# Token couplings folded into VectorE's updates: tanh + ratio times the values, then an addition with a factor

## The reference

```python
gf = _global_net(x.mean(axis=1, keepdims=True), ...)      # one number per batch
out = x
for _ in range(3):
    tf = _coupling_net(out, ...)                          # one number per token
    combined = 0.7 * gf + 0.3 * tf
    coupling = 0.1 + adaptive_range * (combined - 0.5) * 2.0
    out = out + coupling * _twist(out)                    # _twist permutes feature quarters, with signs
```

## Time and profile before

| what | value |
|---|---|
| median of 3 runs | 1072.22 us (1072.2 to 1073.6) |
| the profiled execution's own time | 1072.12 us |
| its span (first to last instruction) | 1070.2 us |
| what lies around the span | 1.9 us |
| mean granted TensorE clock | 0.983 of full speed |
| instructions | 21910 |

### The profile page before, as it was taken

The page is one execution under the profiler, slowest core; times in us unless marked ns, Lnnn a source line. Parts: engine busy times, 40 slices in busy tenths (PEclk is TensorE's granted clock), DMA queues, the critical chain, the costliest instruction groups (busy, mean ns, idle before and its releaser), DMA issues.

```text
span 1070.2 us, 21910 instructions
## 1 busy us (share of the span) xinstructions
PE 977.3 (91%) x7260; PEld 526.2 (49%) x7260; DVE 843.8 (79%) x1770; ACT 901.5 (84%) x1121; POOL 573.9 (54%) x1053
## 2 busy tenths in 40 slices
PE   6899999999899999999999999999989999996993
PEld 4456435554355544555445543555435554454431
DVE  3888796997879886987869879699796988688485
ACT  3999778997799978998789977899779997895575
POOL 3366604876068740887228870487606874087204
PEclk7999999999999999999999999999999999999897
DMA  5433002430033200432005310153002430020002
GB/s 118 88 59 58 6 2 44 103 88 1 1 75 89 71 1 1 98 89 48 1 1 118 88 30 1 36 112 88 0 2 69 92 74 1 2 54 31 11 1 80
DMA packets 191119, 51.71 MB, mean 48 GB/s; under 512 B 165920, under 2 KB 174624, under 8 KB 191008
## 3 DMA queue, kind: packets, MB, share of 16 engines
q1 hardware_dynamic: 191008, 50.31, 22.2%
HBM read 33.37 MB, written 16.78 MB: 47 GB/s over the span
## 4 chain that ended last, share of the span: by engine, by line
PE 43%; DVE 16%; POOL 14%; ACT 13%; issue 10%; SPq 2%; DMA 1%; DVEq 0%; POOLq 0%; ACTq 0%
PE ps L1255 8%; PE ps L1269 7%; PE ps L1239 6%; PE ps L1159 5%; ACT probs L914 5%; PE ps L1190 4%; ACT probs L920 3%; PE ps L1175 3%; POOL f_hat L470 3%; PE ps L1278 2%; POOL twisted L525 2%; DVE move_u L780 2%; DVE move_u L801 2%; DVE move_v L782 2%; POOL q_hat L449 2%
## 5 line engine op out<-in xcount | busy, mean ns | idle before, releaser
L914 ACT ACTIVATE probs<-ps,u_scale 120x2048 f32<-120x2048 f32 x128 | 253.7, 1982 | 23.2 <-PE ps L1159 23.2
L920 ACT ACTIVATE probs<-probs,exp_bias,clip 120x2048 f32<-120x2048 f32 x128 | 270.2, 2111 | 0.1
L1269 PE MATMUL ps<-h,w 128*128 128x512 f32 x384 | 185.5, 605 | 14.5 <-ACT h L948 13.8
L1159 PE MATMUL ps<-q_t,k_t 32*120 32x256 f32 x2048 | 148.9, 405 | 21.5 <-ACT probs L914 20.6
L489 POOL TENSOR_TENSOR c<-tok_c 128x16 f32<-128x16 f32 x8 | 1.8, 223 | 277.8 <-issue 277.8
L1190 PE MATMUL ps<-wo_t,of_t 128*128 128x256 f32 x512 | 143.5, 403 | 1.0 <-DVE xy L717 1.0
L692 DVE STREAM_TRANSPOSE o_t<-ps 128x512 f32<-128x512 f32 x128 | 90.6, 708 | 68.0 <-PE ps L1175 67.7
L1175 PE MATMUL ps<-probs,va 120*32 120x256 f32 x2048 | 138.7, 389 | 1.6 <-ACT probs L920 1.5
L1159 PEld LDWEIGHTS ps<-q_t,k_t 32*120 32x120 f32 x2048 | 93.4, 180 | 58.7 <-issue 51.4
L1269 PEld LDWEIGHTS ps<-h,w 128*128 128x128 f32 x384 | 67.5, 189 | 93.0 <-issue 66.0
L1190 PEld LDWEIGHTS ps<-wo_t,of_t 128*128 128x128 f32 x512 | 86.9, 189 | 49.9 <-issue 41.7
(11 more groups left out here) (132 smaller groups left out, 1791.5 us busy)
## 6 DMA issues: line engine op xcount, KB each, us to landing
xy<-in_x_dram SPq DMA_DIRECT2D x64, 256.0 KB, 3.3
out_dram<-xy SPq DMA_DIRECT2D x64, 256.0 KB, 2.1
cbuf<-in_ctx_dram SPq DMA_DIRECT2D x64, 120.0 KB, 2.8
va<-in_ctx_dram SPq DMA_DIRECT2D x64, 120.0 KB, 3.6
tok_c<-coup SPq DMA_DIRECT2D x256, 0.5 KB, 2.0
move_v<-in_L_xattn_W_out_dram SPq DMA_DIRECT2D x1, 256.0 KB, 5.2
move_u<-in_L_ffn_cn_w_dram SPq DMA_DIRECT2D x1, 256.0 KB, 3.3
w<-in_L_ffn_cn_w_dram SPq DMA_DIRECT2D x1, 128.0 KB, 3.1
```

Source lines behind the costliest of these rows:

```text
L914: eng.activation(probs[:, b % 2, n * HALF:(n + 1) * HALF, :].rearrange("k h q -> k (h q)"), banks(SCORE_BANK, 4)[0:KEYS, :], ACT.Tanh, sca ...
L920: eng.activation(p, p, ACT.Exp, scale=clip[0:KEYS, 0:1], bias=exp_bias[:, b:b + 1]).then_inc(s_exp, 1)
L1159: last = eng.matmul(banks(SCORE_BANK + r)[0:KEYS, odd * S:(odd + 1) * S], k_t[rows, b % 2, odd, n, :], q_t[rows, b % 2, n, :], start=True, ...
L1269: last = eng.matmul(banks(bank), w2[:, k, :], h1[:, p % 2, k, :], start=(k == 0), stop=(k == EK - 1))
```

## The change

`couple` is gone, and with it `s_coup`. The tanh in `coup` stays as ACT wrote it. Instead, c_tok * tanh + c_batch is written as c_tok * (tanh + c_batch / c_tok). DVE computes the ratio `r_batch` once per stage, multiplies (tanh + ratio) with the values, and adds the product with the factor `ct_safe` (c_tok, moved off zero) or `ct_neg`. Both are SCALAR_TENSOR_TENSOR: one scalar per partition and two tensors. Since the ratio belongs to one batch, a product now covers both halves m of one batch (128 x 2 x 256) and not one half of both batches. The semaphore counts of the products stay the same. SP's row copies wait for `s_th`, ACT's tanh, itself. POOL turns the copied tanh into couplings in three more steps (16 in place of 13). Five one-column DVE operations make the constants, once, in slot 1.

```diff
+        r_batch = sb("r_batch", [P, GROUP])
...
-        COEFS = 13
+        COEFS = 16
...
                 for p in range(UPDATES):
                     (cyc, chunk), turn = slot_of(p), UPDATES * g + p
-                    eng.wait_ge(s_coup, CB * (turn + 1))
+                    eng.wait_ge(s_th, turn + 1)
...
+                by_cycle = [tok_c[:, n, :].rearrange("p (t b) -> p t b", b=GROUP) for n in range(CYCLES - 1)]
+                both = tok_c[:, 0:CYCLES - 1, :].rearrange("p c o -> p (c o)")
+                step(0, both, both, c_tok[:, 0:1], 1.0, ALU.mult, ALU.mult, scalar=True)
+                step(1, by_cycle[0], by_cycle[0], by_batch, ALU.add)
+                step(1, by_cycle[1], by_cycle[1], by_batch, ALU.add)
...
+            def coupling_constants():
+
+                eng.wait_ge(s_vec0, N_WO)
+                eng.tensor_scalar(ct_square[:], c_tok[:], c_tok[:, 0:1], None, ALU.mult).then_inc(s_ct, 1)
+                eng.wait_ge(s_ct, 1)
+                eng.tensor_scalar(ct_least[:], ct_square[:], CT_LEAST ** 2, 2 * CT_LEAST, ALU.is_lt, ALU.mult).then_inc(s_ct, 1)
+                eng.wait_ge(s_ct, 2)
+                eng.tensor_tensor(ct_safe[:], c_tok[:], ct_least[:], ALU.add).then_inc(s_ct, 1)
+                eng.wait_ge(s_ct, 3)
+                eng.tensor_scalar(ct_neg[:], ct_safe[:], -1.0, None, ALU.mult).then_inc(s_ct, 1)
+                eng.reciprocal(ct_inv[:], ct_safe[:]).then_inc(s_ct, 1)
...
-            def couple(g, p):
-
-                turn, chunk = UPDATES * g + p, slot_of(p)[1]
-                eng.wait_ge(s_th, turn + 1)
-                eng.wait_ge(s_gcs, g + 1)
-                for b in range(CB):
-                    c = coup[:, turn % 2, b * S:(b + 1) * S]
-                    eng.tensor_scalar(c, c, c_tok[:, 0:1], c_batch[:, chunk * CB + b:chunk * CB + b + 1],
-                                      ALU.mult, ALU.add).then_inc(s_coup, 1)
+            def shifted(turn, chunk, b, other):
+
+                tok = slice((chunk * CB + b) * S, (chunk * CB + b + 1) * S)
+                return (coup[:, turn % 2, b * S:(b + 1) * S].unsqueeze(1).to_broadcast([P, EK, S]),
+                        r_batch[:, chunk * CB + b:chunk * CB + b + 1], other[:, :, tok], ALU.add, ALU.mult)
...
-                eng.wait_ge(s_coup, CB * (turn + 1))
+                eng.wait_ge(s_th, turn + 1)
+                eng.wait_ge(s_ratio, g + 1)
...
                 eng.wait_ge(s_upd, EK * turn)
                 eng.wait_ge(s_vupd, EK * number)
+                for b in range(CB):
+                    eng.scalar_tensor_tensor(move_u[:, :, b * S:(b + 1) * S], *shifted(turn, chunk, b, v_t)).then_inc(s_mvu, 1)
+                for b in range(CB):
+                    eng.scalar_tensor_tensor(move_v[:, :, b * S:(b + 1) * S], *shifted(turn, chunk, b, f_t)).then_inc(s_mvv, 1)
+                eng.wait_ge(s_mvu, CB * (turn + 1))
+                eng.wait_ge(s_mvv, CB * (number + 1))
                 for m in range(EK):
-                    eng.tensor_tensor(move_u[:, m, :], v_t[:, m, tok], coup[:, turn % 2, :], ALU.mult) \
-                       .then_inc(s_mvu, 1)
-                    eng.tensor_tensor(move_v[:, m, :], f_t[:, m, tok], coup[:, turn % 2, :], ALU.mult) \
-                       .then_inc(s_mvv, 1)
-                    eng.wait_ge(s_mvu, EK * turn + m + 1)
-                    eng.wait_ge(s_mvv, EK * number + m + 1)
-                    eng.tensor_tensor(f_t[:, m, tok], f_t[:, m, tok], move_u[:, m, :], ALU.add).then_inc(s_upd, 1)
+                    eng.scalar_tensor_tensor(f_t[:, m, tok], move_u[:, m, :], ct_safe[:, 0:1], f_t[:, m, tok],
+                                             ALU.mult, ALU.add).then_inc(s_upd, 1)
                 for m in range(EK):
-                    eng.tensor_tensor(v_t[:, m, tok], v_t[:, m, tok], move_v[:, m, :], ALU.subtract) \
-                       .then_inc(s_vupd, 1)
+                    eng.scalar_tensor_tensor(v_t[:, m, tok], move_v[:, m, :], ct_neg[:, 0:1], v_t[:, m, tok],
+                                             ALU.mult, ALU.add).then_inc(s_vupd, 1)
...
                 eng.wait_ge(s_h1, EK * (PASSES * g + p + 1))
                 eng.wait_ge(s_upd, EK * turn)
+                for b in range(CB):
+                    eng.scalar_tensor_tensor(move_u[:, :, b * S:(b + 1) * S], *shifted(turn, chunk, b, v_t)).then_inc(s_mvu, 1)
+                eng.wait_ge(s_mvu, CB * (turn + 1))
                 for m in range(EK):
-                    eng.tensor_tensor(move_u[:, m, :], v_t[:, m, tok], coup[:, turn % 2, :], ALU.mult) \
-                       .then_inc(s_mvu, 1)
-                for m in range(EK):
-                    eng.wait_ge(s_mvu, EK * turn + m + 1)
-                    eng.tensor_tensor(f_t[:, m, tok], f_t[:, m, tok], move_u[:, m, :], ALU.add).then_inc(s_upd, 1)
+                    eng.scalar_tensor_tensor(f_t[:, m, tok], move_u[:, m, :], ct_safe[:, 0:1], f_t[:, m, tok],
+                                             ALU.mult, ALU.add).then_inc(s_upd, 1)
...
                     eng.tensor_scalar(c_batch[:], gth[:], c_glob[:, 0:1], 0.1, ALU.mult, ALU.add).then_inc(s_gcs, 1)
+                    eng.wait_ge(s_gcs, i + 1)
+                    eng.wait_ge(s_ct, 5)
+                    eng.tensor_scalar(r_batch[:], c_batch[:], ct_inv[:, 0:1], None, ALU.mult).then_inc(s_ratio, 1)
                     for p in range(CHUNKS):
-                        couple(i, p)
                         update_both(i, p)
                     for p in range(CHUNKS, UPDATES):
-                        couple(i, p)
                         update_u(i, p)
```

More of the change, by code:

```diff
@@ L42 @@
 TINY = 1e-30
+CT_LEAST = 1e-18
 def xattn_ffn_kernel(nc, x, ctx, mask, W_out, scale, log_C,
@@ L165, in xattn_ffn_kernel @@
         c_batch = sb("c_batch", [P, GROUP])
+        r_batch = sb("r_batch", [P, GROUP])
+        ct_square = sb("ct_square", [P, 1])
+        ct_least = sb("ct_least", [P, 1])
+        ct_safe = sb("ct_safe", [P, 1])
+        ct_neg = sb("ct_neg", [P, 1])
+        ct_inv = sb("ct_inv", [P, 1])
         GT = TT * GROUP
@@ L239, in xattn_ffn_kernel @@
         s_l4, s_th = sem("s_l4"), sem("s_th")
-        s_coup = sem("s_coup")
+        s_ct = sem("s_ct")
         s_mvu, s_upd = sem("s_mvu"), sem("s_upd")
@@ L248, in xattn_ffn_kernel @@
         s_glob, s_gact, s_gcs = sem("s_glob"), sem("s_gact"), sem("s_gcs")
+        s_ratio = sem("s_ratio")
         s_res = sem("s_res")
@@ L501, in coefficients @@
                 c1, c2, c3 = (tok_c[:, n, :] for n in range(CYCLES))
[L502 to L506, removed]
+                by_cycle = [tok_c[:, n, :].rearrange("p (t b) -> p t b", b=GROUP) for n in range(CYCLES - 1)]
[3 more added lines that the diff above has]
+                step(1, by_cycle[1], by_cycle[1], by_batch, ALU.add)
+                step(3, c12[:], c1, c2, ALU.mult)
+                step(3, co_b2[:], c1, c2, ALU.add)
+                step(4, co_a2[:], c12[:], -1.0, 1.0, ALU.mult, ALU.add, scalar=True)
+                step(5, tb(co_b3), tb(co_b2), deviation, ALU.mult)
+                step(6, tb(co_a3), tb(co_a2), deviation, ALU.mult)
                 eng.wait_ge(s_ttok, g + 1)
                 step(0, c3, tok_th[:], c_tok[:, 0:1], 1.0, ALU.mult, ALU.mult, scalar=True)
[L509 to L515, removed]
+                step(9, last_c, last_c, by_batch, ALU.add)
+                step(10, c3b2[:], c3, co_b3[:], ALU.mult)
+                step(10, c3a2[:], c3, co_a3[:], ALU.mult)
+                step(11, a3_r[:], co_a3[:], c3b2[:], ALU.subtract)
+                step(12, b3_r[:], co_b3[:], c3a2[:], ALU.add)
+                step(13, x_fac[:], a3_r[:], 1.0, None, ALU.add, scalar=True)
+                step(13, tb(x_add), tb(a3_r), neg_mean, ALU.mult)
                 assert count == COEFS
@@ L872, in _ @@
                         largest_weight()
+                        coupling_constants()
                 else:
```

## The result

| | median us | runs | profiled execution | span |
|---|---|---|---|---|
| before | 1072.47 | 1072.2 to 1073.6 (4) | 1072.12 | 1070.2 |
| after | 1065.75 | 1065.38 to 1066.73 (4) | 1065.54 | 1063.7 |

The ratio is 0.9937, with a 95% interval of 0.992 to 0.9954. In later measurements of the changed kernel it was 0.9933 (0.992 to 0.9946). So the kernel is faster by 0.6 to 0.7%, with 0.5 and 0.8% as the ends of the intervals.

A forecast was written before the change was run, and what follows sets the result against it. No engine is full; DVE's turns 4 to 6 and the row copies each hold the PE and ACT ring. Stages -6.8 (8 x 0.85), constants +0.3: -6.5 from 1072.12, 1065.6, taken as 1065.7; range 1063.5 to 1067.5.

The forecast's parts named there:

- Pitch and length: DVE's new SCALAR_TENSOR_TENSOR: 0.66 us from start to start (bounds 0.605 and 0.72) and 0.753 us long.
- Rival A: DVE's new instructions are heavier, 0.69 to 0.72 us from start to start: 1067.5 to 1072.5 us; chance 0.17.
- B: Over 0.72 us from start to start in DVE's turns 3 to 7 makes it slower, 1084 to 1088 at 0.80; chance 0.07.
- The turns: DVE's time per feed-forward turn: turns 0 to 3 take 5.65 us (before 5.98), turns 4 to 7 take 3.00 (before 3.18).
- The rows: SP's row copies start on ACT's tanh; turn 4's land at about 407.0 instead of 410.3 us, ending the hold on tanh4(6).
- Both only together: DVE's turns 4 to 6 and SP's row copies each hold the PE and ACT ring; only both changes free it.
- PE late next, slack 0.51 us: At layer2(10), PE and not DVE's f_t comes last, until turn 6's first half has moved by 0.51 us.
- The size per stage: Each feed-forward stage, up to token_tanh, gets 0.85 us shorter; over 8 stages 6.8 us.
- the 0.08 added for PE's tail: Small idles in PE's chain after layer2(10) may give up to 0.15 us more; 0.85 was taken over 0.77.
- The constants: Five tiny DVE operations, run once, about 1 us with turn-arounds: cost 0 to 1.0 us, taken as 0.3.
- What DVE saves or loses in turns 0 and 1 is hidden: Early in the stage waits pass almost only through PE; DVE changes stay hidden under 1.5 us, its idle before turn 2.
- Rival C: DVE's new form reads two f32 tensors at half rate, 1.09 us from start to start: 1206 us; chance 0.12.

The follow-up runs named there:

- the run with late copies: Changed kernel, but SP's row copies wait for the turn's u products on DVE, not ACT's tanh: 1075.09 us, ratio 1.0019.
- the run with early copies: Kernel before, with SP copying ACT's tanh at once and DVE's couplings in their own buffer, updates still TENSOR_TENSOR: 1071.71 us, ratio 0.999.
- two kernels with a faster DVE: Changed kernel with products of turns 5 and 7 in `move_v`: 1064.77 us; with all updates plain TENSOR_TENSOR, without ratio and factor: 1069.11 us.
- the pads: Changed kernel plus an idle TENSOR_TENSOR on DVE ahead of each of turns 4 to 7: 1065.03 us with 128x256, 1073.31 us with 128x512.
- the plain ones: Changed kernel with all DVE updates as plain TENSOR_TENSOR, ratio and factor left out: 1069.11 us, ratio 0.9971.

## Why the prediction was right, by its own steps

- **Pitch and length.** Forecast 0.66 and 0.753 us, measured 0.66 and 0.747 to 0.749. The two rows from which it came, a TENSOR_SCALAR with and a CAST without a scalar, gave 68 ns for what is 61. Rival A's 0.69 to 0.72 and B's over 0.72 didn't come about.
- **The turns.** Turns 4 to 7: forecast 3.00, measured 2.99. Turn 3: forecast 5.65, measured 5.50. The step counted a turn-around between turns 3 and 4 that isn't there: turn 4's first product waits for updates of f_t that lie behind two v_t updates, and the last v_t update is no condition of it (403.96 - 402.63 = 1.33 us, two bare steps of 0.66).
- **The rows.** The hold on tanh4(6) went, as forecast. The reading that the trace's releaser (a product of turn 5) was wrong and the copies were the cause is borne out by the run with late copies, in which the profile names the DMA itself, and by the run with early copies, in which DVE's turns are as long as before and the hold is gone.
- **Both only together.** Shown from both sides: 1075.1 (1071.5 in the profiled execution; the rest is open) with DVE's part alone, 1071.7 with the rows' part alone, 1065.0 with both.
- **PE late next, slack 0.51 us.** Shown, as far as DVE goes: two kernels with a faster DVE gain nothing in the stage's second part, and the pads put the slack at 0.4 to 0.5 us.
- **The size per stage.** Forecast 0.85 us, measured 0.80 in most. layer2(10) was to come 0.77 us earlier and came 0.83 earlier against turn 2's tanh; the 0.08 added for PE's tail didn't come, it took 0.03 back. That the sum came out on the spot (-6.5 of -6.5) is in part luck, as small misses cancel: the stages' 0.80 for 0.85 leave 0.4 us out and 0.3 were lost ahead of turn 2 in two stages, while the fifth and seventh stage gave 0.8 more, because of late copies in the profiled execution of before.
- **The constants.** The sum has +0.3 us for them. The first tanh4 did come 0.3 us later in the two profiled executions, but this mark moves by up to 1.9 us between the variants, so no run shows the term.
- **The step that was missing.** "What DVE saves or loses in turns 0 and 1 is hidden" looked at DVE's own slack only. POOL was not in it, though it is slowed by what DVE runs beside it. The change doubled POOL's q_hat pair (1.27 to 2.53 us in most stages) and ate most of the distance between the low halves and PE: in the kernel before POOL's low halves ended at 381.88 and PE loaded the weights at 383.54, 1.7 us later; now it is 0.4 us. It cost 0.16 us each in the second and the seventh stage, where POOL's pair started some 0.3 and 0.5 us later than elsewhere and PE waited 0.48 us for POOL by name. With updates as dense as the plain ones it would have lost 3.8 of its 7 us there. The time hardly shows this miss, but the step as written was wrong.
- **Rival C** (two f32 sources at half rate, 1206 us) falls: 687 ns for 512 elements with a constant, and 747 with a scalar, stand against the 1.2 us or so that it needs. The Trainium skill's sentence on this form (Vector Engine (DVE) Microarchitecture Reference, Points that are easy to get wrong) doesn't hold for these operations. Its reason is that no read port is left to read the accumulator back, and these use no accumulator; the measurement decides.

## What to carry to other kernels

Ask of each wait in a ring what stands right behind it: removing one of two holds changes next to nothing (33.82 us to the hundredth), removing both gives the gain, and neither can be judged by itself. When an operand passes through an extra step, look at who else waits for that step; the copies that could start at the tanh instead of the coupling were needed as much as the shorter turns. And count POOL when DVE's instructions change: shorter instructions on DVE cost 4 us here, as POOL took longer beside them and PE waited for POOL. That they close gaps in which POOL got through is a guess.

## What the runs showed of the hardware

- SCALAR_TENSOR_TENSOR on 128x512 f32 from SBUF takes the time of TENSOR_TENSOR (687 and 684 ns) with a constant, and 61 ns more with a scalar per partition.
- POOL's TENSOR_SCALAR (128x256, a pair) takes 1.10 us alone, 1.27 beside `couple` and the start of a product, 2.53 beside the new form and 3.59 beside plain TENSOR_TENSOR in a dense row. DVE lost little beside it: its first plain products came 0.61 us apart as elsewhere, and a pair of the new form took 1.57 us instead of 1.41. POOL's TENSOR_TENSOR slowed both: its pair took 3.15 instead of 2.3 us (1.15 to 1.16 each alone), and a pair of DVE's 3.03 instead of 1.41. The Trainium skill, SBUF — State Buffer, Who interferes with whom, says that a VectorE operation with two inputs in SBUF contends with a GpSimd operation that reads SBUF, that the ports they share are an exclusive lock, and that the order of issue decides who blocks. The trace agrees that such pairs delay one another. By its times, which are rough for POOL, it doesn't bear out the order: POOL's pair started 0.03 us ahead of DVE's product, and it was POOL that took longer. That dense plain products kept POOL out longer than the scalar form did, although they are shorter, is not in that rule either, and why POOL gets in sooner between the latter isn't settled here.
